# Decay attention on one core, rewritten in steps of two heads with queries in blocks of 64

## The reference

```python
hid = _layernorm(low + sqrt_beta ** 2 * high + x, ln_w, ln_b)   # low: a causal convolution of 5 taps, high = x - low
q, k, v = (proj(q_w, q_b), proj(k_w, k_b), proj(v_w, v_b))
scores = jnp.einsum('bhqd,bhkd->bhqk', q, k) / jnp.sqrt(jnp.float32(dk))
mask = jnp.tril(jnp.ones((s, s), bool))
p_ = jax.nn.softmax(jnp.where(mask, scores, -1e+32), axis=-1) * mask
distcum = jnp.cumsum(p_, axis=-1)
disttotal = p_.sum(-1, keepdims=True)
dist = jnp.sqrt(jnp.clip((disttotal - distcum) * pos, 0.0))     # pos = |query - key|
gamma = -jax.nn.softplus(gammas)[None]
total_effect = jnp.clip(jnp.exp(dist * gamma), 1e-05, 100000.0)
scores = jnp.where(mask, scores * total_effect, -1e+32)
p = jax.nn.softmax(scores, axis=-1)                             # row 0 of p is then set to zero
out = jnp.einsum('bhqk,bhkd->bhqd', p, v)                       # then the heads side by side @ out_w.T + out_b
```

## Time and profile before

| | us |
|---|---|
| median of 3 runs | 3456.83 |
| lowest and highest | 3451.32, 3473.36 |
| the profiled execution, its own time | 3448.74 |
| its span in the trace | 3446.8 |
| mean granted share of the TensorE clock in it | 0.945 |

### The profile page before, as it was taken

How to read it: one execution, slowest core, us unless ns; L and a number is a source line. 1 busy time by engine, 2 the same in 40 slices (tenths; PEclk the granted TensorE clock), 3 DMA queues, 4 the chain that set the end, 5 groups by cost and what they waited for, 6 DMA issues and landing times. The chain is left out here.

```text
span 3446.8 us, 63508 instructions
## 1 busy us (share of the span) xinstructions
PE 3178.7 (92%) x21487; PEld 2207.0 (64%) x21598; DVE 2279.0 (66%) x4822; ACT 1790.9 (52%) x3588; POOL 1376.8 (40%) x1488
## 2 busy tenths in 40 slices
PE   7995899965999999999979999999999999999676
PEld 6885677743555555555546777777777777777455
DVE  4994677756444444444436888888888888888633
ACT  1441566642333322333315777777777777777542
POOL 5650344431000000000004666666666666666461
PEclk9996899977999999999977999999999999999887
DMA  1110000000000000000000000000000000000002
GB/s 44 39 37 6 2 2 2 2 24 1 1 0 0 0 0 0 0 0 0 0 11 1 1 0 0 0 0 0 0 0 0 0 0 0 0 0 0 3 1 49
DMA packets 30290, 19.39 MB, mean 6 GB/s; under 512 B 24011, under 2 KB 27532, under 8 KB 30181
## 3 DMA queue, kind: packets, MB, share of 16 engines
q0 software_dynamic: 6144, 9.84, 1.2%
q1 hardware_dynamic: 24036, 8.12, 1.0%
HBM read 13.75 MB, written 4.19 MB: 5 GB/s over the span
## 5 line engine op out<-in xcount | busy, mean ns | idle before, releaser
L1245 DVE TENSOR_TENSOR prod<-c_h,act 128x512 f32<-128x512 f32 x352 | 243.3, 691 | 480.9 <-PE c_h L1097 396.8
L1177 ACT ACTIVATE act<-c_h 128x512 f32<-128x512 f32 x352 | 210.1, 597 | 655.8 <-PE c_h L1097 655.8
L1430 POOL TENSOR_TENSOR d_decay<-d_later,d_pos 128x512 f32<-128x512 f32 x256 | 326.0, 1273 | 474.5 <-DVE d_later L1847 474.5
L1124 PEld LDWEIGHTS c_out<-e_w,hid 128*128 128x128 f32 x2816 | 340.6, 191 | 79.5 <-issue 79.3
L1124 PE MATMUL c_out<-e_w,hid 128*128 128x64 f32 x2816 | 388.8, 281 | 0.1
L1847 DVE TENSOR_TENSOR_SCAN d_later<-d_cont,d_ex 128x512 f32<-128x512 f32 x256 | 315.8, 1234 | 49.6 <-ACT d_ex L1712 46.2
L1071 POOL TENSOR_TENSOR x_rest<-flatT,x_hm 64x512 f32<-64x512 bf16 (+1 forms) x33 | 38.1, 1154 | 748.5 <-ACT x_hm L1157 724.6
L1548 PEld LDWEIGHTS d_S<-d_kT,d_qT 8*128 8x128 f32 x2048 | 249.4, 188 | 110.6 <-issue 110.6
L1548 PE MATMUL d_S<-d_kT,d_qT 8*128 8x128 f32 x2048 | 298.4, 285 | 0.0
L1439 POOL TENSOR_TENSOR d_p<-d_p,d_mx 128x512 f32<-128x512 f32 x256 | 266.0, 1039 | 60.0 <-DVE d_mx L1866 58.7
L1542 PE MATMUL d_S<-d_hide,d_ident_b 128*128 128x512 bf16 x1088 | 281.7, 384 | 0.0
(11 more groups left out here) (323 smaller groups left out, 6556.7 us busy)
## 6 DMA issues: line engine op xcount, KB each, us to landing
out_h<-g_Y SPq DMA_DIRECT2D x8, 512.0 KB, 4.0
rows<-in_table,idx POOLq DMA_INDIRECT x128
e_w<-in_e_w SPq DMA_DIRECT2D x2, 704.0 KB
e_w<-in_e_w SPq DMA_DIRECT2D x1, 352.0 KB
d_pos<-in_d_pos SPq DMA_DIRECT2D x1, 256.0 KB
d_cont<-in_d_cont SPq DMA_DIRECT2D x1, 256.0 KB
g_w<-in_g_w SPq DMA_DIRECT2D x3, 64.0 KB, 2.0
d_win<-in_d_win SPq DMA_DIRECT2D x1, 146.2 KB
```

The source lines that it names most:

```text
L1124: last = nc.tensor.matmul(bo[:, b * D:(b + 1) * D], hid[u][:, b * P:(b + 1) * P], w2[:, c, :], start=(c == 0 and b == 0), stop=(c == NCH - ...
L1245: nc.vector.tensor_tensor(prod[u][:], b3[u][:], act1[u][:], ALU.mult).then_inc(S["multiplied"], 1)
L1430: pool.tensor_tensor(decay[u][:], later[u][:, 0:W], pos[:], ALU.mult).then_inc(S["placed"], 1)
```

## The change

The phase is written anew. A step is now two heads (`PAIRS`) of four sequences, 128 steps in all. Queries are cut into halves of 64: the partitions hold the same half of two sequences (2 x 64 queries). For the late half ("long", S=1) all 128 keys stand in the free dimension, for the early half ("short", S=0) only the 64 keys that it can see. So a head of a group takes 2 x 128 + 2 x 64 = 384 columns (`SEG`) instead of 512, and a step's tile is 2 x 384 = 768 wide.

- Scan, product, Ln, the exponentials and the product with the distance are one instruction of 768. The two maxima, the two subtractions, and the scaling are two instructions each, of 512 (long) and 256 (short).
- The decay rate, squared, is multiplied into the distances once, in the setup (`posg`), and the exponential of the decay has the constant scale -1 in place of one from a tile.
- On PE a step has two mask matmuls of 384 bf16 columns, eight fp32 score matmuls (16 rows deep; four of 128 and four of 64 columns) that alternate between two strips of rows, and after them four bf16 matmuls of 512 columns into `d_O` (`WARM`), whose result is overwritten by the values. Each head has three transposes instead of four. The values of four heads are 32 matmuls of 64 columns each, every four in a row in four strips of columns.
- The score banks are two (`bS`, two banks wide each) instead of four: the scores of step K wait for the product of step K-2.
- Norms are made by reductions on DVE, squares on ACT and products on POOL instead of DVE's batch-norm instructions; convolution, values and output of two sequences are one matmul with block-diagonal weights. The biases of queries and keys come from a bf16 matmul of three rows. The setup has 18 loads and more small operations; the steps are all written out, with no loop instruction.

The core of the diff (cut):

```diff
...
-    AGAIN = (4, 6, 6, 3, 3, 3, 3, 6)
...
+    HALF = P // 2
+    SEG = 3 * P
+    NG = NB // GB
+    PAIRS = NH // 2
+    NQ = NG * PAIRS
+    KEEP_V, KEEP_P, KEEP_T = 3, 3, 8
+    WARM = 4
...
+hide_f, hide = m_.sb("d_hide_f", [P, SEG]), m_.sb("d_hide", [P, SEG], BF16)
+ident_b, fill = m_.sb("d_ident_b", [P, P], BF16), m_.sb("d_fill", [P, 512], BF16)
...
+ex, decay = [[m_.sb(f"d_{name}{u}", [P, 2, SEG]) for u in range(2)] for name in ("ex", "decay")]
+later = [m_.sb(f"d_later{u}", [P, 1 + 2 * SEG]) for u in range(2)]
+p2 = [m_.sb(f"d_p2{u}", [P, 2, SEG]) for u in range(KEEP_P)]
+pT = [m_.sb(f"d_pT{u}", [P, SEG]) for u in range(KEEP_T)]
...
+bS = [m_.ps(f"d_S{u}", [P, 2, 512]) for u in range(2)]
...
+FIRST, LAST = -16, NQ + 8
...
+        for K in range(FIRST, LAST + 1):
+            m, j = K // PAIRS, K % PAIRS
+            if step_there(K - 1):
+                u = (K - 1) % 2
+                pool.wait_ge(U["inv_total"], 2 * K)
+                pool.wait_ge(U["placed"], K)
+                pool.tensor_tensor(long(decay[u]), long(decay[u]), wide(rtot[u], 1, P), ALU.mult)
+                pool.tensor_tensor(short(decay[u]), short(decay[u]), wide(rtot[u], 0, HALF), ALU.mult)\
+                    .then_inc(U["scaled"], 1)
+            if step_there(K - 2):
+                u, w = (K - 2) % 2, (K - 2) % KEEP_P
+                pool.wait_ge(U["max2_made"], 2 * (K - 1))
+                pool.tensor_tensor(long(p2[w]), long(p2[w]), wide(mx2[u], 1, P), ALU.subtract)
+                pool.tensor_tensor(short(p2[w]), short(p2[w]), wide(mx2[u], 0, HALF), ALU.subtract)\
+                    .then_inc(U["shifted2"], 1)
...
+                    pool.tensor_tensor(hc[:], H[:, n * GB:(n + 1) * GB, :], over(mean[:], D), ALU.subtract)\
+                        .then_inc(G["centred"], 1)
...
+                    pool.tensor_tensor(hs, hs, cb[:, None, :].to_broadcast([P, GB, D]), ALU.add)\
...
+                    pool.tensor_tensor(hn[:], zb[:], over(rstd2[:], D), ALU.mult).then_inc(G["hn_made"], 1)
...
+                    pool.tensor_tensor(xn[:], hc[:], over(rstd[:], D), ALU.mult).then_inc(G["xn_made"], 1)
+            if step_there(K):
+                u = K % 2
+                h = 2 * j
+                pool.wait_ge(U["scanned"], K + 1)
+                if K >= 2:
+                    pool.wait_ge(U["weighed"], K - 1)
+                pool.tensor_tensor(decay[u][:], later[u][:, 0:2 * SEG].rearrange("p (e s) -> p e s", e=2),
+                                   posg[:, h:h + 2, :], ALU.mult).then_inc(U["placed"], 1)
...
+        def scores(K):
...
+            for e in range(2):
+                nc.tensor.matmul(bS[u][:, e, 0:SEG], ident_b[:], hide[:], start=True, stop=False)
+            for g, S in ((0, 1), (1, 1), (0, 0), (1, 0)):
+                cols = slice(g * P, (g + 1) * P) if S else slice(2 * P + g * HALF, 2 * P + (g + 1) * HALF)
+                keys = slice(g * P + (0 if S else HALF), (g + 1) * P)
+                for e in range(2):
+                    r = slice(STRIP * (j % 2 * 2 + e), STRIP * (j % 2 * 2 + e) + 2 * HD)
+                    last = nc.tensor.matmul(bS[u][:, e, cols],
+                                            qT[s][r, c, (2 * g + S) * P:(2 * g + S + 1) * P],
+                                            kT[s][r, c, keys], start=False, stop=(g == 1 and S == 0))
+            last.then_inc(U["scored"], 1)
...
+        def turn(K, e):
+            w = 2 * K + e
+            pe.wait_ge(U["exped2"], K + 1)
+            if w >= 1:
+                pe.wait_ge(U["pT_kept"], w)
...
+            for t in range(3):
+                last = nc.tensor.transpose(bT[:, t * P:(t + 1) * P], p2[K % KEEP_P][:, e, t * P:(t + 1) * P],
+                                           ident[:])
+            last.then_inc(U["turned"], 1)
...
+        def values(i):
...
+            def weigh_values(g, S):
+                rows = slice(0, P) if S else slice(g * HALF, (g + 1) * HALF)
+                for side in range(2):
+                    b = 2 * g + side
+                    at = (g * P if S else 2 * P) + side * HALF
+                    for e in range(QUAD):
+                        last = nc.tensor.matmul(bO[e * STRIP:(e + 1) * STRIP,
+                                                   b * P + S * HALF:b * P + (S + 1) * HALF],
+                                                vs[rows, b if S else GB + side, QUAD * c + e, :],
+                                                pT[(QUAD * i + e) % KEEP_T][rows, at:at + HALF],
+                                                start=True, stop=True)
+                return last
+
+            weigh_values(0, 0).then_inc(Q["near_done"], 1)
+            weigh_values(0, 1)
+            weigh_values(1, 1)
+            pe.wait_ge(Q["near_done"], i + 1)
+            weigh_values(1, 0).then_inc(Q["attended"], 1)
...
+        for K in range(FIRST, LAST + 1):
+            m, j = K // PAIRS, K % PAIRS
+            i = (K - 5) // 2
+            if step_there(K):
+                scores(K)
+                if quad_there((K - 6) // 2):
+                    pe.wait_ge(Q["attT_kept"], (K - 6) // 2 + 1)
+                for _ in range(WARM):
+                    nc.tensor.matmul(bO[:], ident_b[:], fill[:], start=True, stop=True)
+            if step_there(K - 3):
+                turn(K - 3, 0)
...
-                for _ in range(AGAIN[k % GQ]):
-                    nc.tensor.matmul(bS[u][:], ident_b[:], hide[:, None, :].to_broadcast([P, GB, P]),
-                                     start=True, stop=True)
...
+        def keep_turned(K, e):
+            w = 2 * K + e
+            act.wait_ge(U["turned"], w + 1)
+            if w >= KEEP_T:
+                act.wait_ge(Q["attended"], (w - KEEP_T) // QUAD + 1)
+            nc.scalar.activation(pT[w % KEEP_T][:], bT[:, 0:SEG], ACT.Copy).then_inc(U["pT_kept"], 1)
...
+            if step_there(K - 1):
+                u = (K - 1) % 2
+                act.wait_ge(U["scaled"], K)
+                nc.scalar.activation(decay[u][:], decay[u][:], ACT.Ln, bias=1e-18).then_inc(U["log_done"], 1)
+                act.wait_ge(U["log_done"], K)
+                nc.scalar.activation(decay[u][:], decay[u][:], ACT.Exp, scale=0.5).then_inc(U["root_done"], 1)
+            if step_there(K):
+                act.wait_ge(U["shifted"], 2 * (K + 1))
+                nc.scalar.activation(ex[K % 2][:], ex[K % 2][:], ACT.Exp).then_inc(U["exped"], 1)
+            if step_there(K - 1):
+                u = (K - 1) % 2
+                act.wait_ge(U["root_done"], K)
+                nc.scalar.activation(decay[u][:], decay[u][:], ACT.Exp, scale=-1.0).then_inc(U["decay_made"], 1)
+            if step_there(K - 3):
+                keep_turned(K - 3, 0)
+            if step_there(K - 2):
+                w = (K - 2) % KEEP_P
+                act.wait_ge(U["shifted2"], K - 1)
+                nc.scalar.activation(p2[w][:], p2[w][:], ACT.Exp).then_inc(U["exped2"], 1)
...
-                nc.scalar.activation(decay[u][:], decay[u][:], ACT.Exp, scale=minus_g[:, h:h + 1])\
...
+        link(nc.vector.tensor_tensor(bqk[:], X0[0:3, :], bqk[:], ALU.add))
...
+        nc.vector.tensor_tensor(posg[:], pos[:, None, :].to_broadcast([P, NH, SEG]), over(gam[:], SEG), ALU.mult)\
...
+        for K in range(FIRST, LAST + 1):
+            m, j = K // PAIRS, K % PAIRS
+            if step_there(K):
+                u = K % 2
+                dve.wait_ge(U["scored"], K + 1)
+                if K >= 2:
+                    dve.wait_ge(U["exped"], K - 1)
+                nc.vector.tensor_reduce(mx[u][:, 1], long(bS[u]), AX, ALU.max).then_inc(U["max_made"], 1)
+                nc.vector.tensor_reduce(mx[u][:, 0], short(bS[u]), AX, ALU.max).then_inc(U["max_made"], 1)
+                dve.wait_ge(U["max_made"], 2 * K + 1)
+                if K >= 2:
+                    dve.wait_ge(U["scanned"], K - 1)
+                nc.vector.tensor_tensor(long(ex[u]), long(bS[u]), wide(mx[u], 1, P), ALU.subtract)\
+                    .then_inc(U["shifted"], 1)
+                dve.wait_ge(U["max_made"], 2 * K + 2)
+                nc.vector.tensor_tensor(short(ex[u]), short(bS[u]), wide(mx[u], 0, HALF), ALU.subtract)\
+                    .then_inc(U["shifted"], 1)
...
+            if step_there(K):
+                u = K % 2
+                dve.wait_ge(U["exped"], K + 1)
+                if K >= 2:
+                    dve.wait_ge(U["placed"], K - 1)
+                nc.vector.tensor_tensor_scan(later[u][:, 1:1 + 2 * SEG], cont[:],
+                                             ex[u][:].rearrange("p e s -> p (e s)"), 0.0, ALU.mult, ALU.add)\
+                    .then_inc(U["scanned"], 1)
+                dve.wait_ge(U["scanned"], K + 1)
+                if K >= 2:
+                    dve.wait_ge(U["scaled"], K - 1)
+                sums = later[u][:, 1:1 + 2 * SEG].rearrange("p (e s) -> p e s", e=2)
+                nc.vector.reciprocal(rtot[u][:, 1], long(sums)[:, :, :, P - 1]).then_inc(U["inv_total"], 1)
```

(23 more changed lines are left out.)

862 lines of the change are left out of this document (370 added, 492 removed).

## The result

The kernel after the change takes 3261.69 us (median of 4 runs, 3237.47 to 3278.01) where the kernel before took 3463.64 us beside it: a ratio of 0.941, 95% interval 0.933 to 0.950. It saved about 200 us, where 349 were forecast, and 3262 us lies outside the range (3040 to 3250). Its profiled execution took 3245.55 us.

The account below looks back on a forecast made before the run. PE's queue was taken as the bound, afterwards a ring of waits. 15 + 41 + 1050 + 20 = 1126 us against 1474.7 saves 349: 3448.7 becomes 3100, plus 8 for the median, 3108 us; 8-in-10 range 3040 to 3250.

Parts of the forecast that it names:

- 128 steps are 1050 us: Decay phase after the change: 7.9 us of waits plus 0.3 us port delay make 8.2 us a step, over 128 steps.
- in the steady state I cost them at nothing: Four overwritten matmuls behind a step's scores: hidden by PE's slack of about 1 us; without slack up to 130 us.
- Rival 2: PE's clock falls to 1.2 GHz for the decay phase: PE's 7.0 us a step become 12.6, 3671 us; chance 0.05.
- the sum itself: PE's work in one step after the change, all forms added: 7.0 us, in a step of 8.2 us.
- The ring: Waits from scan through distance product, scaling, Ln, Exp and next softmax exponential to the next scan: 7.9 us a step.
- DVE against POOL: Shared port: POOL's second subtraction and norm products hold DVE's scan by 0 to 0.7 us a step; 0.3 taken.
- Rival 3: The DVE-POOL port costs its upper bound and handovers are 0.1 us: step 8.9 us, time 3200 us; chance 0.08.
- rival 1: PE stays the bound because packing of scores and values fails to overlap: 115 us more, 3225 us; chance 0.22.
- The rule on mode changes: The Trainium skill's statement that a change of tiling mode drains TensorE; no row priced it by itself.
- Ends: Around the decay steps: setup 15 us more, a lead of 41 us before the first scores, about 20 us behind the last step.
- The low end of the range: Bottom of the 8-in-10 range for the whole kernel: no port delay and 5 us of setup, put at 3040 us.

## Why the prediction was wrong

**The failed step.** What failed is the clock in the sum: "128 steps are 1050 us" counts every step of 8.2 us at the full clock. It rests on what I wrote of the four overwritten matmuls, "in the steady state I cost them at nothing; what hides them is PE's slack of about 8 - 7 = 1 us a step". As a cost that holds (twelve instead of eight add 0.11 us a step). But it left their gain at nothing too, and slack of this kind is the pause at which the clock fell. Rival 2 named the mechanism and gave it 0.05, with a price for the whole phase at the low clock alone. The profile had the middle: low for half of the time, with a mean step of 9.46 us, not 12.6, and a stretch of 1228 us. Against the full clock the four places of a group lose 2.27, 2.09, 0.03 and 0.87 us, 5.26 us in 32 groups: 168 us. The error of the stretch is 158. With eight matmuls a step, all else the same, 160 of it are gone, which is why I call the cause shown.

**Rival 2's evidence** was read wrongly. That block attention holds 1.00 with PE busy for 286 of 300 us was evidence at 95%; the sum itself gave 7.0 of 8.2 us, 85%, and no row before showed a clock at that share. The earlier trace rows even had a counter-example: 98% busy at 0.64 from 1800 to 1850 us. The kernel before without its repeats, TensorE busy for 97%, has 0.82, so even a share as high as block attention's would have been no evidence.

**The ring** was right. With eight matmuls the stretch is 1068 us, forecast 1070, and the step 8.14 us, forecast 8.2. Its rows in that kernel, a timeline over one step (from VectorE's, GpSimd's and ScalarE's answers):

```profile
2520.59 1.76 DVE L1827 TENSOR_TENSOR_SCAN d_later<-d_cont,d_ex 128x768 f32<-128x768 f32 x1 [0.36 <-ACT d_ex L1621]
...
2528.50 1.76 DVE L1827 TENSOR_TENSOR_SCAN d_later<-d_cont,d_ex 128x768 f32<-128x768 f32 x1 [1.26 <-ACT d_ex L1621]
```

```profile
2522.43 1.81 POOL L1428 TENSOR_TENSOR d_decay<-d_later,d_posg 128x768 f32<-128x768 f32 x1 [1.84 <-DVE d_later L1827]
2524.38 1.04 POOL L1379 TENSOR_TENSOR d_decay<-d_decay,d_rtot 128x512 f32<-128x512 f32 x1
2525.37 0.61 POOL L1380 TENSOR_TENSOR d_decay<-d_decay,d_rtot 128x256 f32<-128x256 f32 x1
```

```profile
2526.02 0.84 ACT L1616 ACTIVATE d_decay<-d_decay 128x768 f32<-128x768 f32 x1 [2.50 <-POOL d_decay L1380]
2526.89 0.84 ACT L1618 ACTIVATE d_decay<-d_decay 128x768 f32<-128x768 f32 x1
2527.64 0.83 ACT L1621 ACTIVATE d_ex<-d_ex 128x768 f32<-128x768 f32 x1
```

From scan to scan 7.91 us, each piece as priced.

**DVE against POOL.** The size came out, the cause did not, so that 8.14 us meet 8.2 is in part luck. No scan was held: in all 128 steps of the change they take 1758 to 1761 ns. In the step above, GpSimd has done its norm products by 2520.58 us, when the scan starts at 2520.59, and is idle for 1.84 us until the scan is over.

The collision did come, but once in a group and the other way round. In the first step of a group GpSimd's subtraction of the mean (0.61 us where no scan runs) starts 0.02 us behind the scan and ends 0.41 us after it:

```profile
2503.92 1.76 DVE L1827 TENSOR_TENSOR_SCAN d_later<-d_cont,d_ex 128x768 f32<-128x768 f32 x1 [0.63 <-ACT d_ex L1621]
...
2503.94 2.15 POOL L1402 TENSOR_TENSOR d_hc<-H,d_mean 128x256 f32<-128x256 f32 x1
```

This happens in 27 of the 32 groups with eight, and in 8 of the 32 of the change. The distance product then starts 0.37 us behind the scan instead of 0.08. It had no price here: with eight, first steps take 8.53 to 8.63 us with it, and one without it takes 8.53. The Trainium skill's rule of the exclusive port ("SBUF — State Buffer", "SBUF: two separate sides") says that whichever of the two starts first has it for the whole instruction; the 2.15 us agree. I had asked only what the scan loses. I also read the earlier trace rows loosely: DVE's product ended 1.08 us after POOL's (3427.04 against 3425.96 us), not with it.

The 0.2 us over 7.9 come from the first two steps of a group: in the first, TensorE has projection and convolution, and VectorE waits 1.27 us for the next scores. Rival 3 falls.

**Packing, rival 1.** Score records at full clock are 89 and 70 ns (forecast 72), value records 27 and 20 ns (forecast 35): 1.3 and 0.8 us a step for 1.2 and 1.1. The rule on mode changes cost nothing that I can find. With the scores' overlap gone and the values' hardly touched, the whole costs 77 us; the rival had 115 for both. What the values' packing is worth stays open.

**Ends.** The first norm came 19.4 us later (forecast 15), the first mask 26.5 us behind it (41). The median lies 16 us above the profiled execution, not 8. In the sum: +4 - 15 + 158 = +147 us, and 3245.6 - 3100 = 146. The low end of the range was mis-added as well: no port delay and 5 us of setup make 3108 - 38 - 10 = 3060 us, not 3040.

## What to carry to other kernels

An edit that takes work from TensorE, or idle-looking matmuls out of its queue, also takes what kept its clock up; look at the pauses that the new schedule leaves and, as one timeline above suggests, at stretches of narrow matmuls (few rows or columns), and price a half-low clock too, not only all or nothing. Where TensorE has slack, try the number of filler matmuls (0, 4, 8, 12 here: 3333, 3262, 3087, 3103 us): too many is cheap, too few is dear. Here they did most where they kept the clock up for the step with TensorE's densest work.
